# Four convolution layers on a 16 x 2048 x 2048 map: a narrower covariance split, one spread on another engine, a unit later in the order, two tiles per transfer

## The reference

```
def _gn(v, G=8, eps=1e-5):      # mean and variance over 2 channels x 2048 x 2048
    ...
    return ((g - m) / jnp.sqrt(s + eps)).reshape(v.shape)
# conv: for each of the 15 partitions of {i0, i1, o0, o1} one term
Yi = einsum(X, weights[i]) / denom     # 16 -> 16 channels
Y = sum of Yi + sum(bias)
```

## Time and profile before

| | |
|---|---|
| median of 3 runs | 2004.12 us (2001.9 to 2005.36) |
| the profiled execution | 2002.07 us |
| its span, first to last instruction | 1999.8 us |
| PE busy | 1619.5 us (81%) |
| DVE busy | 1328.4 us (66%) |
| POOL busy | 261.1 us (13%) |
| ACT busy | 84.0 us (4%) |
| moved | 834.80 MB, mean 417 GB/s |

### The profile page before, as it was taken

One profiled execution on the slowest core, in us unless ns is written; L12 is line 12 of the kernel. 1 busy time (PEld: TensorE's weight loads), 2 busy tenths in 40 slices (PEclk: granted clock), 3 DMA queues, 4 the chain that ended last, 5 costly groups with the idle time before them and its releaser, 6 DMA issues.

```text
span 1999.8 us, 43443 instructions
## 1 busy us (share of the span) xinstructions
PE 1619.5 (81%) x19825; PEld 988.2 (49%) x19825; DVE 1328.4 (66%) x1269; ACT 84.0 (4%) x91; POOL 261.1 (13%) x497
## 2 busy tenths in 40 slices
PE   6888888888888889999777777777877777777873
PEld 6877778777777754443333333333333333333331
DVE  5988888888888855676555555555555555555552
ACT  0110111110111120000000000000000000000000
POOL 7333333333332320000000000000000000000000
PEclk9999999999999999999999999999899999999897
DMA  9999999999999994999999999999999999999998
GB/s 376 417 412 412 422 422 422 422 422 422 422 422 421 422 426 210 383 430 430 431 431 429 432 431 431 430 430 431 431 430 431 431 430 430 431 431 431 430 431 364
DMA packets 78957, 834.80 MB, mean 417 GB/s; under 512 B 10616, under 2 KB 10744, under 8 KB 11320
## 3 DMA queue, kind: packets, MB, share of 16 engines
q1 hardware_dynamic: 59208, 564.75, 67.2%
q10 hardware_dynamic: 19696, 269.40, 31.5%
HBM read 564.73 MB, written 269.09 MB: 417 GB/s over the span
## 4 chain that ended last, share of the span: by engine, by line
another core or an unknown queue 48%; DMA 33%; PE 9%; DVE 6%; SPq 2%; issue 0%; ACT 0%; POOL 0%; DVEq 0%
DMA early<-pairs 28%; PE ps L813 6%; DVE ring_own L545 5%; DMA out<-ring_own 2%; SPq L317 2%; DMA early<-strip_in 1%; DMA dia_in<-dia 1%; PE ps L714 1%; PE ps L821 0%; PE ps L820 0%; PE ps L740 0%; PE ps L741 0%; SPq L326 0%; PE ps L794 0%
## 5 line engine op out<-in xcount | busy, mean ns | idle before, releaser
L813 PE MATMUL ps<-ring_own,mixer 128*128 128x512 f32 x1252 | 593.9, 632 | 134.9 <-DMA ring_own<-strip_in 105.3
L689 PE MATMUL ps<-early 128*64 128x66 f32 x17408 | 591.4, 225 | 122.1 <-DMA early<-pairs 112.3
L545 DVE TENSOR_REDUCE ring_own<-early 128x32 f32<-128x2048 f32 x272 | 619.7, 2285 | 82.7 <-DMA early<-pairs 82.1
L689 PEld LDWEIGHTS ps<-early 128*64 128x64 f32 x17408 | 555.8, 139 | 157.5 <-DMA early<-pairs 128.2
L660 DVE SCALAR_TENSOR_TENSOR ring_own<-ps,row_sum,stage 128x512 f32<-128x512 f32 (+3 forms) x233 | 301.5, 1294 | 317.2 <-PE ps L813 317.2
L813 PEld LDWEIGHTS ps<-ring_own,mixer 128*128 128x128 f32 x1252 | 247.6, 202 | 481.6 <-issue 436.2
L813 PE MATMUL ps<-early,mixer 128*128 128x512 f32 x800 | 377.7, 629 | 87.1 <-DMA early<-strip_in 65.7
L660 DVE SCALAR_TENSOR_TENSOR early<-ps,row_sum,stage 128x1024 f32<-128x1024 f32 (+2 forms) x152 | 192.5, 1266 | 197.9 <-PE ps L813 197.9
L813 PEld LDWEIGHTS ps<-early,mixer 128*128 128x128 f32 x800 | 157.4, 201 | 307.0 <-issue 278.1
L375 POOL TENSOR_TENSOR gram_all<-gram_all,stage 128x1024 f32<-128x1024 f32 x68 | 150.0, 2205 | 0.0
L668 DVE SCALAR_TENSOR_TENSOR ring_own<-ps,row_sum,stage 128x488 f32<-128x488 f32 (+43 forms) x308 | 133.3, 474 | 0.0
(11 more groups left out here) (139 smaller groups left out, 119.2 us busy)
## 6 DMA issues: line engine op xcount, KB each, us to landing
early<-pairs SPq DMA_DIRECT2D x272, 1056.0 KB, 18.1
ring_own<-strip_in SPq DMA_DIRECT2D x78, 2048.0 KB, 23.3
out<-ring_own ACTq DMA_DIRECT2D x78, 2048.0 KB, 63.3
early<-strip_in SPq DMA_DIRECT2D x50, 2048.0 KB, 23.3
out<-early ACTq DMA_DIRECT2D x50, 2048.0 KB, 64.5
const<-const_f SPq DMA_DIRECT2D x1, 773.5 KB, 22.0
ring_own<-dia_pair SPq DMA_DIRECT2D x1, 640.0 KB, 21.9
ring_own<-half_in SPq DMA_DIRECT2D x1, 512.0 KB, 37.1
```

Source lines behind the costliest of these rows:

```text
L545: nc.vector.tensor_reduce(part_sum[:, t % sums], vbuf[:, s].rearrange("p (q w) -> p q w", w=FOUR)[:, :, 0:PAIR * SUB].rearrange("p q (c a) ...
L689: last = mm(regions(parity)[lane:lane + WIDE, m // BANK_REGIONS, m % BANK_REGIONS], chunk(slot, k, WIDE), chunk(slot, k, WIDE + MARKS), st ...
L813: last = mm(ps[:, first + at // BANK, 0:piece], mixer[:, :, :].rearrange("p a m -> p (a m)"), buf[:, at:at + piece], start=True, stop=True)
```

## The change

1. The covariance of a block is one matmul of 80 columns, and so are its corrections, in place of one of 64 and one of 16.
2. The last block's spread (L575) is done by GpSimd in the last `add_quad`, between the row sums and the 128x1024 addition, with a semaphore of its own (`spread_late`), and VectorE no longer does it.
3. The unit with d = 9 stands at place 13 of the order, behind those with d = 10, 11 and 12, for loads, matmuls and outputs.
4. TensorE's wait for `f2_done` in layer 1 stands behind the first two matmuls of the layer, and the three spins before these are left out in layer 1.
5. Tiles are laid out in twos; one load brings two tiles (16,896 bytes in a row for each partition), there are four semaphores for the eight slots, and a load waits until both tiles of its two slots are done.

```
-    return v.reshape(len(tiles), BLK, VW), *as_units(...)
+    v = v.reshape(len(tiles) // 2, 2, BLK, VW).transpose(0, 2, 1, 3)
+    return np.ascontiguousarray(v).reshape(len(tiles) // 2, BLK, 2 * VW), *as_units(...)
...
     units.insert(4, (half_strip,))
+    units.insert(13, units.pop(10))
...
-            for t in range(len(tiles)):
+            for t in range(0, len(tiles), 2):
+                s = t % V_SLOTS
                 if t >= V_SLOTS:
-                    sp.wait_ge(gram_done, t - V_SLOTS + 1)
-                    sp.wait_ge(summed, t - V_SLOTS + 1)
-                sp.dma_start(vbuf[:, t % V_SLOTS], v[t]).then_inc(v_in[t % V_SLOTS], 16)
-                if t == V_SLOTS - 1:
+                    sp.wait_ge(gram_done, t - V_SLOTS + 2)
+                    sp.wait_ge(summed, t - V_SLOTS + 2)
+                sp.dma_start(early[:, s * VW:(s + 2) * VW], v[t // 2]).then_inc(v_in[s // 2], 16)
+                if t == V_SLOTS - 2:
...
                 last.then_inc(rows_added, 1)
+                if q == len(spans) - 1:
+                    pool.wait_ge(rows_added, len(spans))
+                    pool.wait_ge(matrices_in, 16 * 13)
+                    nc.gpsimd.tensor_tensor(spread[:, late], row_sum[:, late]..., c("v_sub")..., ALU.mult).then_inc(spread_late, 1)
                 if q:
                     pool.wait_ge(gram_added, q)
...
-            dve.wait_ge(rows_added, len(spans))
             dve.wait_ge(matrices_in, 16 * 13)
-            tt(spread[:, late], row_sum[:, late]..., c("v_sub")..., ALU.mult).then_inc(to_pe, 1)
...
             spin(3, 1)
-            pe.wait_ge(to_pe, 1)
+            pe.wait_ge(spread_late, 1)
             by_rows(nb // 2).then_inc(from_pe, 1)
...
             for b in range(nb):
-                mm(cov[0:64], f1[:, b, 0:64], f1[:, b], start=b == 0, stop=False)
-                mm(cov[64:FEATS], f1[:, b, 64:], f1[:, b], start=b == 0, stop=False)
+                mm(cov, f1[:, b], f1[:, b], start=b == 0, stop=False)
...
-            mm(cov[0:64], m80[:, 1, 0:64], m80[:, 0], start=False, stop=False)
+            mm(cov, m80[:, 1], m80[:, 0], start=False, stop=False)
             pe.wait_ge(rs_done, 1)
-            mm(cov[0:64], c("gram_p")[:, 0:64], rs[:, 0], start=False, stop=True)
-            mm(cov[64:FEATS], c("gram_q")[:, 64:], rs[:, 1], start=False, stop=True).then_inc(from_pe, 1)
+            mm(cov, c("gram_p"), rs[:, 0], start=False, stop=False)
+            mm(cov, c("gram_q"), rs[:, 1], start=False, stop=True).then_inc(from_pe, 1)
...
             for layer in range(LAYERS):
-                if layer == 1:
-                    pe.wait_ge(f2_done, 1)
-                if layer:
+                if layer > 1:
                     spin(3, 7)
                 pe.wait_ge(to_pe, pe_in)
                 mm(ps[0:ROWS, 0, 0:1], c("centre"), state[:, FEATS:], start=True, stop=True)
                 mm(ps[0:ROWS, 1, 0:FEATS], state_t[:, :], phi[:, :], start=True, stop=True).then_inc(from_pe, 1)
+                if layer == 1:
+                    pe.wait_ge(f2_done, 1)
                 if layer:
                     spin(3, 7)
```

More of the change, by code:

```diff
@@ L85, in lay_out @@
                 z[q, :, h, :, at:at + width] = a[:, SUB * g:SUB * g + SUB, j:j + width].transpose(1, 0, 2)
-    return v.reshape(len(tiles), BLK, VW), *as_units(z.reshape(len(strips(n)), BLK, n))
+    v = v.reshape(len(tiles) // 2, 2, BLK, VW).transpose(0, 2, 1, 3)
+    return np.ascontiguousarray(v).reshape(len(tiles) // 2, BLK, 2 * VW), *as_units(z.reshape(len(strips(n)), BLK, n))
 def as_units(z):
@@ L281, in regions @@
             return half.rearrange("p b (m w) -> p b m w", m=BANK_REGIONS)
+        late = slice(groups // 2, groups // 2 + per_block)
         dia_acc = ps[0:FEATS, 0, 512 - FEATS:512]
@@ L293, in chunk @@
             return rows[:, k // COLS, 0:width, k % COLS]
-        v_in = [sem(f"v_in{s}") for s in range(V_SLOTS)]
+        v_in = [sem(f"v_in{s}") for s in range(V_SLOTS // 2)]
         z_in = [sem(f"z_in{s}") for s in range(TWOS + 1)]
@@ L301, in build @@
         gram_staged, gram_added, rows_added = sem("gram_staged"), sem("gram_added"), sem("rows_added")
-        spread_early, rs_done, ones_done = sem("spread_early"), sem("rs_done"), sem("ones_done")
+        spread_early, spread_late = sem("spread_early"), sem("spread_late")
+        rs_done, ones_done = sem("rs_done"), sem("ones_done")
         place_done, matrices_in, beta_done = sem("place_done"), sem("matrices_in"), sem("beta_done")
@@ L372, in add_quad @@
                 last.then_inc(rows_added, 1)
+                if q == len(spans) - 1:
+                    pool.wait_ge(rows_added, len(spans))
+                    pool.wait_ge(matrices_in, 16 * 13)
+                    nc.gpsimd.tensor_tensor(spread[:, late], row_sum[:, late].unsqueeze(2).to_broadcast([BLK, per_block, SUB]),
+                                            c("v_sub").unsqueeze(1).to_broadcast([BLK, per_block, SUB]),
+                                            ALU.mult).then_inc(spread_late, 1)
                 if q:
@@ L541, in _ @@
                 s = t % V_SLOTS
-                dve.wait_ge(v_in[s], 16 * (t // V_SLOTS + 1))
+                dve.wait_ge(v_in[s // 2], 16 * (t // V_SLOTS + 1))
                 if t >= sums:
@@ L571, in _ @@
                     link(tt(dia_cov[:, :], dia_cov[:, :], c("blocks"), ALU.mult))
-            late = slice(groups // 2, groups // 2 + per_block)
-            dve.wait_ge(rows_added, len(spans))
             dve.wait_ge(matrices_in, 16 * 13)
-            tt(spread[:, late], row_sum[:, late].unsqueeze(2).to_broadcast([BLK, per_block, SUB]),
-               c("v_sub").unsqueeze(1).to_broadcast([BLK, per_block, SUB]), ALU.mult).then_inc(to_pe, 1)
             dve.wait_ge(sum_added, len(tiles))
@@ L585, in _ @@
                                     ALU.add).then_inc(to_pe, 1)
-            dve.wait_ge(to_pe, 2)
+            dve.wait_ge(to_pe, 1)
             dve.wait_ge(from_pe, 2)
@@ L603, in _ @@
             tt(phi[:, :], phi[:, :], dia_cov[:, :], ALU.add).then_inc(to_pe, 1)
-            pe_in, pe_out = 5, 3
+            pe_in, pe_out = 4, 3
             for layer in range(LAYERS):
@@ L685, in quad @@
                     opens, closes = slot % QUAD == 0, slot % QUAD == QUAD - 1
-                    pe.wait_ge(v_in[slot], 16 * (turn + 1))
+                    if slot % 2 == 0:
+                        pe.wait_ge(v_in[slot // 2], 16 * (turn + 1))
                     for k in range(CHUNKS):
@@ L730, in _ @@
             spin(3, 1)
-            pe.wait_ge(to_pe, 1)
+            pe.wait_ge(spread_late, 1)
             by_rows(nb // 2).then_inc(from_pe, 1)
             spin(6, 1)
-            pe.wait_ge(to_pe, 2)
+            pe.wait_ge(to_pe, 1)
             mm(ps[:, 2, 0:3 * CH], c("mean"), feat_sum[:, :], start=True, stop=True).then_inc(from_pe, 1)
             spin(9, 1)
-            pe.wait_ge(to_pe, 3)
+            pe.wait_ge(to_pe, 2)
             cov = ps[0:FEATS, 3, 0:FEATS]
             for b in range(nb):
-                mm(cov[0:64], f1[:, b, 0:64], f1[:, b], start=b == 0, stop=False)
-                mm(cov[64:FEATS], f1[:, b, 64:], f1[:, b], start=b == 0, stop=False)
-            pe.wait_ge(to_pe, 4)
+                mm(cov, f1[:, b], f1[:, b], start=b == 0, stop=False)
+            pe.wait_ge(to_pe, 3)
             mm(ps[0:ROWS, 0, 0:1], mean_row[:, :], one, start=True, stop=True)
             mm(ps[0:FEATS, 0, 1:2], m80[:, 0], one, start=True, stop=True)
-            mm(cov[0:64], m80[:, 1, 0:64], m80[:, 0], start=False, stop=False)
+            mm(cov, m80[:, 1], m80[:, 0], start=False, stop=False)
             pe.wait_ge(rs_done, 1)
-            mm(cov[0:64], c("gram_p")[:, 0:64], rs[:, 0], start=False, stop=True)
-            mm(cov[64:FEATS], c("gram_q")[:, 64:], rs[:, 1], start=False, stop=True).then_inc(from_pe, 1)
+            mm(cov, c("gram_p"), rs[:, 0], start=False, stop=False)
+            mm(cov, c("gram_q"), rs[:, 1], start=False, stop=True).then_inc(from_pe, 1)
             spin(3, 1)
-            pe_in = 5
+            pe_in = 4
             for layer in range(LAYERS):
-                if layer == 1:
-                    pe.wait_ge(f2_done, 1)
-                if layer:
+                if layer > 1:
                     spin(3, 7)
```

## The result

The changed kernel takes 1980.88 us in the median of 4 runs (1978.71 to 1988.4), the kernel before 2004.48 us beside it: a ratio of 0.9887 (95% interval 0.9871 to 0.9902), 23.6 us faster by the medians. The profiled execution took 1981.7 us, its span is 1979.9 us, 19.9 less than before's 1999.8.

What follows compares the result with a forecast made beforehand. Transfers bound both stages, so time is bytes over rate plus DMA idle. Tiles -6.5, chain -4.6 and filled gaps -7.4 sum to -18.5 us, from the median of 2004.12 to 1985.6 us; range 1978 to 1994.

Steps and rivals of the forecast that it cites:

- the idle behind the tiles: Between tile stage and steady outputs, DMA engines lack work: 20 us before the first output, then 7.0 from 784 to 806.
- Tiles: Tile stage: two tiles per transfer, longer pieces read at 426 GB/s instead of 422, -6.5 us.
- the rule of the Trainium skill on packets: Tile stage rival: each packet costs a fixed small time, so -3.9 us for -6.5, 1988.2 us; chance 0.12.
- The last pair: End of tile stage: both tiles arrive only with the second, leaving VectorE two reduces before the features, +2.3 us.
- The spread: Chain behind the tiles: spread on GpSimd starts the late rows' matmuls earlier, -1.25 us; VectorE additions may stand, +0.3 us.
- the stall that was feared: Chain: one of VectorE's two additions may stand beside GpSimd's tree, 0 to 1 us, taken as +0.3.
- The covariance: Chain: 16 blocks as 32 passes of 80 columns, at the transposes' 0.12 us each, -4.6 us.
- The wait for the copies: Layer 1: wait for the features' copy moved behind the first two matmuls, -1.3 us.
- The order: Behind the first output: three loads ahead of the features' unit fill idle DMA time, -7.4 us.
- The payback at unit 19: Later load into the features' buffer: DMA waits 2 us in each of four units, 1993.0 us; chance 0.06.
- the clock: Shorter chain: TensorE's granted clock falling from its full level would show the prediction wrong; no size or chance given.

Runs made afterwards that it cites:

- e1: The kernel before with only the tiles laid out and loaded in twos: 1998.68 us, ratio 0.9972.
- e5: The changed kernel with one transfer for two tiles, but the tiles in HBM as before, in pieces of 8,448 bytes: 1987.94 us, ratio 0.9921.
- e3: The kernel before with only the covariance in 80 columns: 1997.29 us, ratio 0.9962.
- e4: The changed kernel with the covariance back in 64 and 16 columns: 1987.09 us, ratio 0.9919.
- e2: The kernel before with only the features' unit moved to place 13 of the order: 1995.89 us, ratio 0.9963.
- e9: The kernel before run once more, unchanged, one execution: 2002.5 us.
- e10: The changed kernel run once more, unchanged, one execution: 1986.07 us.
- e7: The changed kernel with three more spins in layer 0, between its first two pairs of matmuls: 1981.64 us, ratio 0.9885.
- e12: As e7, with more spins in the middle's waits except the two around layer 1's first two matmuls: 1979.54 us, ratio 0.9869.
- e6: The changed kernel with each pair of tiles in two transfers of 64 partitions, pieces of 16,896 bytes: 2654.09 us, ratio 1.3256.
- e8: As e7, with the last pair in two transfers and TensorE's last turn written out behind its loop: 1984.37 us, ratio 0.9898.

## Why the prediction was right

The forecast was 1985.6 us, range 1978 to 1994, and the measured 1980.88 lies in it. The two causes, bytes over rate and the idle behind the tiles, are the ones that the runs show. For the profiled execution the same sum gave 1983.6 us, and 1981.7 was measured; that these are so near is in part luck, since 4.1 us that the sum lacked (2.7 in the tiles, 1.4 in the covariance) stand against 3.0 of a slow clock that it hadn't priced. Its steps:

**Tiles.** Forecast -6.5 us at 426 GB/s, measured 428 in the changed kernel and in e1, and 9.2 and 8.4 us. The mechanism holds, by e5 against the changed kernel: the piece's length alone gives or takes it. The term was too small by 2.7 us: 426 came from 34 us of units with pieces of 16,384 bytes, while 422 and 428 are means over 490 us. The estimate from the rule of the Trainium skill on packets (DMA: Bandwidth & Descriptors, "Why small descriptors are slow (HBM only)"), 3.9 us, lies further off; the trace doesn't agree with its size.

**The last pair.** +2.3 forecast, +1.9 in e1.

**The spread.** -1.25 and +0.3 forecast. From the last tiles to the late row sums it is 7.84 us in e1 and 6.50 in the changed kernel, -1.34: the spread takes 0.40 us on GpSimd and is ready 0.5 us ahead of TensorE. From there to the covariance it is 4.91 us and was 4.64, +0.27: L599, the second of VectorE's two additions, takes 0.68 us beside GpSimd's tree where 0.44 had been usual. That is the stall that was feared, at its small end, in the changed kernel:

```profile
714.26 0.95 DVE L596 TENSOR_TENSOR f<-f,ps 128x768 f32<-128x768 f32 x1 [0.58 <-PE ps L743]
715.25 0.42 DVE L598 TENSOR_TENSOR f<-f 128x256 f32<-128x256 f32 x1
...
715.26 0.72 POOL L475 TENSOR_TENSOR gram_all<-gram_all 128x128 f32<-128x128 f32 x1
...
715.59 0.68 DVE L599 TENSOR_TENSOR f<-f 128x256 f32<-128x256 f32 x1
```

L598 started 0.01 us ahead of the tree's last addition and kept its 0.42 us; this addition took 0.72 us where it takes 0.46 in the kernel before, and L599 stood behind it. The Trainium skill (SBUF — State Buffer, "Who interferes with whom") has it so, for VectorE instructions with two SBUF inputs beside a GpSimd instruction that reads SBUF; L596, with one SBUF input and beside the tree too, keeps the 0.95 us that it takes in the kernel before. No run undoes the spread alone, so its part of the time is read from these timelines only.

**The covariance.** -4.6 forecast. The 16 blocks take 718.77 - 716.32 = 2.45 us for 8.40, -5.95, or 0.077 us a pass, not the transposes' 0.12. The term was short by 1.4 us: the transposes move 128 columns, the covariance 80, and 0.077 to 0.12 is nearly as 80 to 128. e3 and e4 give 7.2 and 6.2 us for the whole edit.

**The wait for the copies.** -1.3 forecast; the state is ready at 727.52 and L769 comes at 729.17: 1.65 us for 2.94, -1.29.

**The order.** -7.4 forecast, 7.7 by the idle in the profile, 8.6 in e2. Over all profiles the time behind the first output is 7.2 us shorter by the means. The payback at unit 19 didn't come: DMA's share is 1.00 and more there.

**What wasn't in the sum** is the clock, 3.0 us in this profile. It had been named as a thing that would make the prediction wrong, with no price. The sum of the chain's parts is 1.91 - 1.34 + 0.27 - 5.95 - 0.16 (what stands behind the covariance) - 1.29 = -6.6 us, and 3.0 of it went to the slow clock. I took that first for the price of the short covariance; e9 showed a fall of the same size in the kernel before, and e10 a larger one elsewhere in the changed kernel. The kernel before had just been profiled without one. By that the profiles' difference (19.9 us) would understate the change and the medians' (23.6) be nearer; but e9 had its fall and no longer span, so this isn't shown. The single parts' medians add up to 5.9 + 8.6 + 7.2 = 21.7, and the spread and the copies' wait are left with 1.9, where the traces have 1.07 + 1.29. Each of the three is known to some 3 us only, so this contradicts nothing and shows little.

What stays open: why the clock falls in one execution and not in another. Most falls came behind places where TensorE stood for 0.6 to 1.7 us, but e4 has such places and no fall, and e10's longest began at about 749 us with TensorE busy for 4.00 of 4 us from 744 to 748 and again from 748 to 752. More work in layer 0's (e7, e12) was followed by a full clock there and a fall in layer 1, behind its two waits; a kernel with these filled too wasn't run. That the fills moved the fall isn't shown either, as e10 has it in the same place without them.

## What to carry to other kernels

Where transfers bound both stages, look at the hole between them and at the order in which one queue waits: a load that waits for something late holds all loads behind it, and one line that puts it three places back gave 8.6 of 23.6 us. Where the queue is kept full, make a partition's contiguous piece longer before making transfers fewer (e5); and when a chain of small matmuls is measured, look at the granted clock in each execution before giving a microsecond to an edit.

## What the runs showed of the hardware that was not expected

- The piece's length still counts at 8 KB: 428 GB/s with 16,896 bytes and 422 with 8,448, whether a transfer brings one tile or two (before, e5), at a DMA share of 1.01 in all.
- Transfers of 64 partitions each, two behind one another on one queue, read 219 GB/s at share 1.01, half of the rate (e6). The Trainium skill (SBUF — State Buffer, "Door 1: The DMA port swizzle") says that partitions 0 to 63 reach 8 of the 16 ports, with some 218 GB/s as the limit; this run agrees. The same page ("Can I just issue two DMAs to hit both halves?") says that two such transfers serialize, and the pairs of them here read no more than that page gives for one; the whole kernel took 1.3 times as long.
- Two matmuls of 64 and 16 columns in turn cost 0.131 us a pass, and one of 80 columns 0.077: splitting a weight matrix by width made each pass slower, not only more of them.
- TensorE's granted clock fell to its lower level in the middle chain in 11 of 13 profiles (e6 left out; all but the first of before and e4), for some 3 to 14 us in all and not always at the same place. The first output came 56.1 to 61.1 us after the last tiles in five profiles with the changed chain or nearly so (changed kernel, e5, e7, e10, e12). Without a fall it would be about 54.6, an estimate: e4 has 60.6 and no fall, and its covariance takes 5.95 us longer.
- Code written out behind a loop on TensorE had one stop of 2.04 us that no record of another engine explains (e8).
